# Two groups of context products moved among the results of the last two sets, in an attention block on one core

## What is computed

```python
q = _heads(seq_inputs @ Wq + bq)
k = _heads(seq_inputs @ Wk + bk)
v = _heads(seq_inputs @ Wv + bv)
scores = jnp.einsum('bhqd,bhkd->bhqk', q, k) / np.sqrt(HEAD_SIZE)
bias = jnp.where(graph_mask, 0.0, NEG)[:, None]
probs = jax.nn.softmax(scores + bias, axis=-1)
ctx = jnp.einsum('bhqk,bhkd->bhqd', probs, v)
ctx = ctx.transpose(0, 2, 1, 3).reshape(seq_inputs.shape[0], seq_inputs.shape[1], H)
return ctx @ Wf + bf
...
x = _layernorm(x + _L0_gnn_ref(x, ...), axis=-1)
```

## Time and profile before

| | us |
|---|---|
| median of 3 runs (990.02 to 991.3) | 990.89 |
| the profiled execution, whole | 993.77 |
| its span, from first to last instruction | 991.9 |
| PE busy in it | 983.5 |
| DVE / ACT / POOL busy | 705.0 / 642.4 / 617.4 |

### The profile page before, as it was taken

How to read it: one execution, slowest core, us unless ns; L and a number is a source line. 1 busy time by engine, 2 the same in 40 slices (tenths; PEclk the granted TensorE clock), 3 DMA queues, 4 the chain that set the end, 5 groups by cost and what they waited for, 6 DMA issues and landing times.

```text
span 991.9 us, 26953 instructions
## 1 busy us (share of the span) xinstructions
PE 983.5 (99%) x7638; PEld 905.0 (91%) x7638; DVE 705.0 (71%) x2526; ACT 642.4 (65%) x2103; POOL 617.4 (62%) x636
## 2 busy tenths in 40 slices
PE   9999999999999999999999999999999999999997
PEld 8889898998989989899898998989999898998996
DVE  5555768586686866868677686776867778585796
ACT  4777739558395673947749476484865739558564
POOL 2232757656676676656776577765776757656584
PEclk9999999999999999999999999999999999999998
DMA  7567674866658566684756848568495674856665
GB/s 177 103 147 175 183 218 125 231 156 199 195 147 227 155 195 184 164 230 127 215 175 178 228 103 236 166 186 220 110 246 148 191 209 128 234 175 196 212 201 190
DMA packets 346953, 180.61 MB, mean 182 GB/s; under 512 B 229024, under 2 KB 330528, under 8 KB 346912
## 3 DMA queue, kind: packets, MB, share of 16 engines
q1 hardware_dynamic: 344848, 178.74, 65.7%
q10 hardware_dynamic: 2064, 1.38, 0.5%
HBM read 104.53 MB, written 75.50 MB: 181 GB/s over the span
## 4 chain that ended last, share of the span: by engine, by line
PE 96%; SPq 1%; DMA 1%; DVE 0%; issue 0%; POOL 0%; POOLq 0%; DVEq 0%
PE scores_ps L549 18%; PE scores_ps L550 18%; PE scores_ps L551 18%; PE scores_ps L706 9%; PE scores_ps L597 8%; PE scores_ps L607 5%; PE work_ps L549 4%; PE work_ps L551 4%; PE work_ps L550 4%; PE work_ps L706 3%; PE work_ps L607 3%; PE work_ps L597 1%; SPq L367 1%; DMA p_out<-p_turned 1%; PE work_ps L775 0%
## 5 line engine op out<-in xcount | busy, mean ns | idle before, releaser
L1199 ACT ACTIVATE probs<-probs,neg_max 128x128 f32<-128x128 f32 x768 | 297.0, 391 | 22.3 <-DVE neg_max L893 22.3
L1423 POOL TENSOR_TENSOR probs<-probs,inv_sum 128x768 f32<-128x768 f32 x128 | 204.3, 1622 | 100.0 <-DVE inv_sum L920 96.2
L1418 POOL TENSOR_SCALAR x_in<-x_in,mean_var,rstd 128x384 f32<-128x384 f32 x108 | 178.5, 1653 | 20.5 <-POOL rstd L1408 20.5
L912 DVE STREAM_TRANSPOSE p_turned<-probs 128x768 f32<-128x768 f32 x124 | 120.8, 974 | 79.6 <-DMA p_out<-p_turned 66.8
L893 DVE CUSTOM_DVE_ANT_0 probs<-scores_ps,mask_bias 128x128 f32<-128x128 f32 x640 | 137.8, 286 | 46.4 <-PE scores_ps L597 46.3
L1408 POOL TENSOR_TENSOR rstd<-var_eps,minus_half 128x1 f32<-128x1 f32 x116 | 65.0, 560 | 143.3 <-DVE var_eps L956 143.1
L1199 ACT ACTIVATION_READ_ACCUMULATOR probs<-probs,neg_max 128x1 f32 x768 | 145.8, 190 | 0.0
L1214 ACT COPY v_next<-scores_ps 128x384 f32<-128x384 f32 x92 | 44.0, 480 | 142.8 <-PE scores_ps L551 141.7
L1402 POOL TENSOR_TENSOR x_in<-x_in,bias_row 128x384 f32<-128x384 f32 x116 | 114.3, 1015 | 0.0
L880 DVE TENSOR_TENSOR xT_lo<-xT,xT_hi 128x768 fp32r<-128x768 f32 x62 | 74.4, 1237 | 45.9 <-ACT xT_hi L1180 45.8
L549 PE MATMUL scores_ps<-wv_hi,xT_hi 128*128 128x384 f32 x282 | 94.6, 336 | 0.0
(11 more groups left out here) (171 smaller groups left out, 2490.3 us busy)
## 6 DMA issues: line engine op xcount, KB each, us to landing
pT<-p_out SPq DMA_DIRECT2D x508, 96.0 KB, 2.9
p_out<-p_turned SPq DMA_DIRECT2D x124, 384.0 KB, 3.0
x_blocks<-in_x SPq DMA_DIRECT2D x372, 64.0 KB, 2.3
x_in<-in_x SPq DMA_DIRECT2D x116, 192.0 KB, 2.8
out<-x_in SPq DMA_DIRECT2D x116, 192.0 KB, 1.9
adj_u<-in_adj SPq DMA_DIRECT2D x32, 64.0 KB, 2.2
x_blocks<-in_x SPq DMA_DIRECT2D x4, 192.0 KB, 4.0
xT<-in_x SPq DMA_DIRECT2D x4, 192.0 KB, 3.5
```

What stands on the lines that cost most here:

```text
L912: nc.vector.transpose(turned(s, e).rearrange("p b h j -> p h b j"), probs[:, e, :, :].rearrange("p h (b k) -> p h b k", b=BLOCKS)).then_in ...
L1199: last = nc.scalar.activation(probs[:, e, h, :], probs[:, e, h, :], ACT.Exp, bias=neg_max[:, e, h:h + 1], scale=-1.0, accum_out=row_sum[:, ...
L1418: nc.gpsimd.tensor_scalar(x_slot(n, e), x_slot(n, e), mean_var[:, at, 0:1], rstd[:, at, 0:1], ALU.subtract, ALU.mult).then_inc(y_ready, 1)
L1423: nc.gpsimd.tensor_tensor(probs[:, e, :, :], probs[:, e, :, :], inv_sum[:, e, :].unsqueeze(2).broadcast_to([P, HEADS, SEQ]), ALU.mult).the ...
```

## The change

Only the ending is touched. PE: context (15,0) stands ahead of result (14,7) instead of behind it, and context (15,1) behind results (15,0) and (15,1) instead of ahead of them. DVE: the three splits of context (15,0) stand ahead of the adds of (14,6) and (14,7) and of the statistics of (14,3). ACT: the casts of context (15,0) stand ahead of the first eight normalisings instead of between the first four and the next. No instruction is added or taken away, and POOL's and SP's orders stay.

```diff
@@ PE, ending
-                for e in range(SET):
+                for e in range(7):
                     out_product(LAST - 1, e)
-                for half in range(2):
-                    ctx_group(LAST, half)
-                for e in range(SET):
+                ctx_group(LAST, 0)
+                out_product(LAST - 1, 7)
+                for e in (0, 1):
+                    out_product(LAST, e)
+                ctx_group(LAST, 1)
+                for e in range(2, SET):
                     out_product(LAST, e)
@@ DVE, ending
-                for e in (1, 2, 3):
+                for e in (1, 2):
                     find_parts(s - 1, e)
                     join_parts(s - 1, e - 1)
                     add_residual(s - 1, e + 3)
-                join_parts(s - 1, 3)
-                add_eps(s - 1, 0, GROUP)
                 for m in range(KC):
                     split_ctx(s, 0, m)
-                add_residual(s - 1, 7)
+                for e in (6, 7):
+                    add_residual(s - 1, e)
+                find_parts(s - 1, 3)
+                for e in (2, 3):
+                    join_parts(s - 1, e)
+                add_eps(s - 1, 0, GROUP)
                 find_parts(s - 1, 4)
@@ ACT, ending
-                for n in BY_SCALAR[:GROUP]:
-                    normalise_late(n)
                 for m in range(KC):
                     round_ctx(s, 0, m)
-                for n in BY_SCALAR[GROUP:2 * GROUP]:
+                for n in BY_SCALAR[:2 * GROUP]:
                     normalise_late(n)
```

## The result

The changed kernel takes 992.02 us (median of 22 runs, 991.49 to 992.68) against 990.39 for the kernel before in the same runs (989.57 to 993.24): 1.6 us more, a ratio of 1.0015 with an interval of 1.0008 to 1.0021. Forecast was 989.6. Yet its profiled execution is 1.1 us shorter than that of before, 992.68 against 993.77 with a span of 990.8 against 991.9. The changed kernel's profiled execution is itself the longest of its 22 runs, 0.66 above their median.

The account below looks back on a forecast made before the run. TensorE was busy 983.5 of 991.9 us, but DVE was taken to end the kernel. First add of set 15 0.13 us later, chain behind it 1.47 shorter: 1.3 less, median 990.89 to 989.6; range 988.3 to 992.0.

Parts of the forecast that it names:

- Before it was 975.72: DVE, kernel before: the profiled start of set 15's first residual add, from which the forecast counted 0.13 us later.
- T0: DVE: start of the first residual add of set 15, result (15,0); forecast 975.85 after the change.
- the two gaps and the slow clock: PE, context (15,1): waits before images 6 and 7, 2.0 us, and slow matmuls behind, 1.8 us; all forecast to go.
- the chain: DVE, from set 15's first add to the last var_eps: 12.52 us before, forecast 11.05 without waits for PE.
- 970.4 forecast for context (15,1): PE: results (15,0) and (15,1) end at 970.4, then context (15,1) follows, with 0.9 us of margin on image 7's landing.
- the slow matmuls: PE, image 7's passes and the first result behind them at the lower clock: claimed to cost 1.8 us.
- 6 us ahead of DVE's last var_eps: Sign of being right: PE's last matmul near 982.5, this far before DVE's final var_eps.
- The 0.1 us of late casts: ACT: normalisings run to 973.05, so casts of context (15,1), with data there at 972.95, start at most 0.1 late.
- The 0.1 us of margin of result (15,0): PE: the split of context (15,0) is done at 967.1, just before result (14,7) ends at 967.2.
- rival C: DVE's second scaled_mean blocked by POOL's bias additions through the shared port lock: 990.3; chance 0.08.
- Rival A: Image 7 lands earlier in the median's runs, which the new order can't use: up to 2.5 us slower, 993.4; chance 0.13.
- Rival B: Image 7 lands later in the median's runs, costing only the old order: gain up to 2.2, 988.6; chance 0.24.

Follow-up runs that it names:

- before_again: The kernel before, unedited, profiled once more: 991.21 us beside a reference median of 990.78, span 989.4.
- before_third: The kernel before, unedited, profiled a third time: 990.81 us beside a reference median of 990.87, span 989.0.
- before_nowait: The kernel before, with images 6 and 7 in context (15,1) multiplying image 5's probabilities and awaiting only its landing: 989.66 us against 990.78, ratio 0.9985.
- after_late: The changed kernel with three small DMAs on SP ahead of image 7's loads: 992.38 us, ratio 1.0015 to the kernel before.
- after_nowait: The changed kernel, with images 6 and 7 in context (15,1) multiplying image 5's probabilities and awaiting only its landing: 992.26 us against 990.87, ratio 1.0014.
- act_late: The changed kernel with ACT's casts of context (15,1) ahead of normalising (14,0) to (14,3): 992.16 us against 990.61 for the kernel before, ratio 1.0016.
- both: The changed kernel with the edits of dve_early and act_late together: 989.84 us, ratio 0.9994 to the kernel before.
- before_late: The kernel before with three small DMAs on SP ahead of image 7's loads: 993.83 us against 990.78, ratio 1.0024.
- dve_early: The changed kernel with DVE's adds and statistics of (15,0) and (15,1) ahead of the splits of context (15,1): 990.13 us against 990.61 for the kernel before, ratio 0.9994.

## Why the prediction was wrong
**The failed step is the starting point, "Before it was 975.72".** That T0, and the two gaps and the slow clock ahead of it, belonged to one execution that took 2.9 us more than the median. The prediction took a difference inside it, 1.3 us, off a median made of other executions. In the usual one T0 stands at 973.65 and 973.35 (before_again, before_third). By before_again the sum reads: T0 from 973.65 to 976.17, 2.52 later; the chain from 12.05 (985.70 - 973.65) to 10.93 (987.10 - 976.17), 1.12 shorter; together 1.40 us more. Measured were 1.6.

These profiles don't reach the ending at the same time. The start of context (14,0) in the first profile of before, the changed kernel, before_again and before_nowait:

```profile
943.11 3.71 PE L607 MATMUL scores_ps<-pT,v_sb 128*64 128x128 f32 x64
...
943.43 3.71 PE L607 MATMUL scores_ps<-pT,v_sb 128*64 128x128 f32 x64
...
943.03 3.71 PE L607 MATMUL scores_ps<-pT,v_sb 128*64 128x128 f32 x64
...
943.24 3.71 PE L608 MATMUL scores_ps<-pT,v_sb 128*64 128x128 f32 x64
```

From there to the last var_eps it is 45.13 us in the first profile, 42.67 in before_again (42.46 in before_third), 41.12 in before_nowait, and 43.67 in the changed kernel (43.66 in after_late, after_nowait and act_late). So the new ending is 1.46 shorter than the one that the prediction read, 1.0 to 1.2 longer than the usual one, and 2.55 longer than one without a gap.

**Within that execution the steps held.** PE: 970.4 forecast for context (15,1), 970.94 in a profile that runs 0.3 later from before the ending on (context (14,0) starts at 943.43 instead of 943.11). No gap, no slow clock, PE done 3.3 us earlier, 3.6 without the offset, against 3.8 forecast. T0 975.85 forecast, 976.17 measured, 975.85 when the 0.32 is taken off. The chain 11.05 forecast, 10.93 measured. Last var_eps 986.9 forecast, 987.10 measured. Span 1.1 shorter against 1.3. Two slips of the prediction did no harm. By its own rows the slow matmuls cost 1.7 us ((1.48 - 0.7) + (2.56 - 1.65)), not 1.8, a term that the sum doesn't use. And its sign "6 us ahead of DVE's last var_eps" should read 4.3 by its own times (986.9 - 982.6); measured were 4.1.

**ACT's and DVE's middle.** ACT's second four normalisings started at 971.00 against 970.65, the offset again, and the cast stood directly behind them. The 0.1 us of late casts that it allowed for came to 0.03 (act_late). The 0.1 us of margin of result (15,0) was enough: there is no wait of PE for it. scaled_mean took 0.17 in both places, so rival C did not come. Had it met the bias additions it would have cost 0.66, as both shows, near the 0.75 taken.

**Rival A was the true case, too rarely weighed at 0.13 and sized too large at 2.5.** Its mechanism is right: the new order can't use an early landing (after_nowait), the old one can (before_nowait, 1.1 us). Its size (from 984.3 to 986.9 is 2.6) holds for no gap at all (2.55 above); the usual execution has a gap of 1.05 us, and before_again ends 1.3 later than before_nowait does (985.70 against 984.36). Only that extreme was priced, "over 992.9"; the half-way case, which came, was put to the other rivals without a time. What was held against A looked at the wrong leg: the 2.4 us from issue to landing of the loads was indeed the same in before_again (2.3), but the wait for the store ahead of them, taken as given, was the 2.0 us that varied. The prediction named the 2.9 us between profile and median as its evidence and then priced the forecast as if they lay elsewhere; its last sentence says that the whole would be wrong if the runs behind the median didn't have those gaps, and they didn't. The change did stay within 0.2%, but on the other side, and just past the end of the range (992.02 against 992.0), which the prediction had cut to leave A out.

**Rival B** was the right mechanism for the wrong runs: before_late and after_late show it, with 3.1 us against none for 1.5 us of delay.

**What stays open:** why the store of image 6's probabilities took 6.8 us in the first profile and 4.8 in before_again; and 0.4 to 0.6 us between the 1.0 to 1.2 of the endings and the 1.6 of the medians. An estimate for the latter: by medians the gap costs the old order 1.1 us (before_nowait), in the two usual profiles 1.34 and 1.55 (42.46 and 42.67 less 41.12). If the median execution loses only the 1.1, the change costs 2.55 - 1.1 = 1.45. No profile shows such an execution.

## What to carry to other kernels
Before a gap in a profile is priced, put the profiled execution's time beside the median: if it is longer by more than the change could win, the gap may be what makes it longer, and a second profile tells. Compare two profiles from a common point close ahead of what was changed, not from the start of the span. A wait on a DMA is a time that varies, and filling it with work that must come first trades it for a fixed delay; the fill pays only if what the waiting step releases is not the start of the last chain. Where one engine's idle time is filled, move the consumer's work too: here DVE had 2.5 us of idle and two results ready, and using them gave back what the move had cost (2.1 us by the traces of dve_early and both), though no more than level with the kernel before is shown.

## What the runs showed of the hardware
One gap of 1.05 us of PE left the granted clock at 1.00; two gaps of 1.15 and 0.86 with twelve passes between, and one of 2.86, were followed by 0.50 for about 3 us, in which a matmul of 384 columns took 0.52 to 0.69 instead of 0.34. So a landing later by 1.1 us (971.48 against 970.39) moved T0 by 2.1. One and the same store of 384 KB kept the loads behind it waiting for 4.2 to 5.2 us in thirteen profiles and for 6.8 in one. A scaled_mean of 128x4 took 0.83 to 0.92 us beside POOL's bias additions and 0.17 without them.
